# Attention inside a fused layer: a scaled projection moved to ScalarE and GpSimd, one more key block turned by VectorE, and the gather spread over all heads

## The chip, the cores and the metric

The kernel runs on one core of one Trainium2 chip. The metric is the time of one execution on the device, in microseconds (us). Besides that time there is one profiled execution, whose trace gives every instruction's start and duration on each engine: PE (TensorE; PEld is its weight load), DVE (VectorE), ACT (ScalarE), POOL (GpSimd) and SP (SyncE, which here only issues DMAs).

## What is computed

The reference takes x of 2 x 2048 tokens of width 256, normalises each token, and adds to x an attention (16 heads of width 64) and a mixture of experts (32 experts, 8 for each token, and a shared one):

```python
xn = _layernorm(x)
# attention
scores = jnp.einsum('bqhk,bshk->bhqs', Q, K) / jnp.sqrt(64)
attn   = jax.nn.softmax(scores, axis=-1)
out_h  = jnp.einsum('bhqs,bshk->bqhk', attn, V)
attn_out = jnp.einsum('bqhk,hdk->bqd', out_h, W_O) + b_O
# experts: the 8 best of 32 by sigmoid score, weights w normalised to 2.5
routed = sum over the 8 of w * down(silu(min(g, 7)) * clip(u, -7, 7))
shared = silu(xn @ shared_gate.T) * (xn @ shared_up.T) @ shared_down.T
return x + attn_out + routed + shared
```

All inputs are float32.

## The kernel before, in words

The program has three stages, each a block of five engine programs with a barrier at its end: `project_and_route` (Q, K and V, split into a high and a low part where scores need it, the routing, and a "base" of x, biases and shared expert, all written to device memory), `run_experts`, and `attend` (from L786), in which three quarters of the time goes.

`attend` walks over 2 batches x 16 heads x 16 query tiles of 128 queries, 512 slots in all. `slots` (L852) says what each slot does, `over_heads` (L874) unrolls head 0 and head 15 of each batch and runs heads 1 to 14 in a loop of one head a trip. Four tiles make a group (`GT`). The engines work on different tiles at one time. In a slot s:

- PE: `transpose` (L1033) turns the last 4 key blocks (`TURNED`) of the probabilities of tile s-2 into PSUM bank 7 (`TURN_BANK`). `score` (L1013) makes the 128 x 2048 scores of tile s in two halves of 1024, with 8 matmuls. `project` (L1062) multiplies the output of a tile 13 slots back with W_O into the same bank 7. `times_v` (L1047) multiplies probabilities with V for a whole group of 512 queries: in each slot 4 of the 16 key blocks, in the order of quarters `PV_ORDER = (3, 0, 1, 2)`, so that the four slots of a group are its places 0 to 3. V is only 64 wide, so even key blocks use columns 0 to 63 of the array and odd ones 64 to 127 (`side = t % 2 * DH`, L1056).
- DVE: two maxima over 1024 scores (`maximum`, L1132), the negated maximum (L1141), then one `scalar_tensor_tensor` (L1178) that takes the projection out of bank 7, scales it by 1/sum and adds it to the accumulator `acc`, then `turn_blocks` (L1146), a 32x32 block transpose of the first 12 key blocks (`MOVED`). Once a group come the sum and its reciprocal (L1188, L1191).
- ACT: exp of the second half (`exponent`, L1099), the copy of the 4 turned blocks (`take`, L1092), exp of the first half, and once a group the copy of the finished output (L1124).
- SP: all loads of q, k, v and W_O, and `exchange` (L913): 16 DMAs a group that move DVE's 32x32 blocks between partitions. Keys are loaded twice a head, once for each half of the tiles (`next_k`, L895).
- POOL: a loop that gathers the 8 expert rows of each token tile from device memory (L959), scales and adds them (L980, L983). It runs by itself through batch 1's 16 tiles, which go into the accumulator of batch 1, and then batch 0's, which go by way of device memory; at the end of batch 0 POOL adds them and stores the output (L1003, L1005).

The order around the changed parts is set by waits. PE's `transpose` of a slot waits until the projection before it has been taken out of bank 7: `wait_pos(pe, added, ...)`. So it waits for DVE's L1178, which stands behind both maxima. ACT's second-half exp waits for the negated maximum; PE's second half of scores waits for that exp.

Of the kernel before, what the change touches and what calls it, by code (L numbers as in the profile page):

```python
# [13 lines left out]
P = 128  # L14
# [578 lines left out]
def run_experts(nc, io, scr, keep, ahead, start):  # L593
    with ExitStack() as stack:
# [27 lines left out]
        @block.sync  # L622
        def _(sp):
            def load(i):
                for q in range(2):
                    e = 2 * i + q
                    wait_apart(sp, turned, 2 * i + q - 1, sp_waits)
                    wait_apart(sp, gu_ready, 2 * i + q - 1, sp_waits)
                    wait_apart(sp, dn_kept, 2 * i + q - 1, sp_waits)
                    load_expert(sp, io, scr, ahead, e, q)  # L630


            load_k(sp, scr, start, 0, 0, 0)
            load_q(sp, scr, start, 0, 0, 0)
            with sp.Fori(1, E // 2) as i:
                load(i)
# [123 lines left out]
MOVED = 12  # L760
# [4 lines left out]
PV_ORDER = (3, 0, 1, 2)  # L765
# [14 lines left out]
def load_k(sp, scr, start, b, h, side):  # L780

    sp.dma_start(start["k_hl"][:, side, :].bitcast(F32), scr["k"][bass.ds(h * P, P), b * T:(b + 1) * T]
# [3 lines left out]
def attend(nc, io, scr, keep, ahead, start):  # L786
    with ExitStack() as stack:
# [9 lines left out]
        acc_last = ahead["xe"][:, 1, :, :]  # L797
# [4 lines left out]
        acc_first = m.sb("acc", [P, TILES - CAP // P, D])  # L802
        acc_second = m.sb("acc_second", [P, TILES, D])
# [8 lines left out]
        rows = ahead["gu"][:, :, :, :].rearrange("p q k o -> p (q k) o")  # L812
        rest = m.sb("rest", [P, D])
        rest_t = rows[:, 0:2, :]
# [18 lines left out]
        cleared = m.sem("cleared")  # L833
        added = m.sem("added")
        rest_loaded = m.sems("rest_loaded", 2)
        finished = m.sem("finished")
        stored = m.sem("stored")
        restarted = m.sem("restarted")
        out_stored = m.sem("out_stored")
        g_staged = m.sem("g_staged")  # L840
        g_base = m.sem("g_base")
        gathered = m.sem("gathered")
        g_step = m.sem("g_step")
        g_stored = m.sem("g_stored")
        sp_waits, pool_waits = m.sem("sp_waits"), m.sem("pool_waits")
        block = stack.enter_context(nc.Block())

        def acc(b, t):

            if b == 1:  # L850
                return acc_second[:, t, :]
            return acc_first[:, t, :] if t < TILES - CAP // P else acc_last[:, t - (TILES - CAP // P), :]  # L852

        def slots(b, h):


            head = b * H + h
            opens = b == 0 and isinstance(h, int) and h == 0
            for s in range(LAST if b == B - 1 and isinstance(h, int) and h == H - 1 else TILES):
# [6 lines left out]
                    s=s, head=head, tile=tile, scores=s < TILES,  # L866
# [22 lines left out]
        def _(sp):  # L889
# [5 lines left out]
            def next_k(b, h, side):  # L895
                head = b * H + h
                wait_apart(sp, late_scored, (head - 1) * TILES + (side + 1) * TILES // 2, sp_waits)
                load_k(sp, scr, start, b, h, side)

            def load_v(b, h, place):  # L900
                wait_apart(sp, pv_done, GT * ((b * H + h) * GROUPS - 1) + place + 1, sp_waits)
                quarter = PV_ORDER[place]
                tiles = slice(quarter * GT, (quarter + 1) * GT)
                sp.dma_start(v[:, tiles, :],
                             scr["v"][bass.ds(h, 1), :, b * NS + quarter * GT:b * NS + (quarter + 1) * GT, :]
                             .rearrange("a p t c -> p (a t) c")).then_inc(v_loaded[quarter], 16)

            def load_wo(b, h, side):
                wait_apart(sp, projected, (b * H + h) * TILES - TILES // 2 * (1 - side), sp_waits)
# [13 lines left out]
            def head_loads(b, h, before, following):  # L923

                next_q(b, h, 1)
                next_k(b, h, 1)
# [5 lines left out]
                load_wo(b, h, 0)  # L932
# [3 lines left out]
                if following is not None:  # L936
                    next_k(*following, 0)
                exchange(b, h, 1)
                if following is not None:
                    next_q(*following, 0)  # L940
                exchange(b, h, 2)
                load_wo(b, h, 1)

            for b in range(B):
                head_loads(b, 0, (b - 1, H - 1) if b else None, (b, 1))
                with sp.Fori(1, H - 1) as h:
                    head_loads(b, h, (b, h - 1), (b, h + 1))
                head_loads(b, H - 1, (b, H - 2), (b + 1, 0) if b + 1 < B else None)
            exchange(B - 1, H - 1, GROUPS - 1)
            for t in range(TILES):  # L950
                sp.wait_ge(added, (B * H - 1) * TILES + t + 1)
                sp.dma_start(io["out"][(NT - TILES + t) * P:(NT - TILES + t + 1) * P, :], acc(1, t)
                             ).then_inc(out_stored, 16)
# [3 lines left out]
        def _(pool):  # L957
            def gather(k):
                nc.gpsimd.indirect_dma_start(  # L959
                    out=rows[:, k % 4, :], out_offset=None, in_=scr["ye"][:, :],  # L960
                    in_offset=bass.IndirectOffsetOnAxis(ap=g_index[:, k:k + 1], axis=0),
                    bounds_check=SLOTS, oob_is_err=True).then_inc(gathered, 16)

            def routed(i, tile):

                nc.gpsimd.tensor_copy(g_index[:, :], keep["index"][:, bass.ds(tile, 1), :]
                                      .rearrange("p a k -> p (a k)"))
                nc.gpsimd.tensor_copy(g_gain[:, :], keep["gain"][:, bass.ds(tile, 1), :]
                                      .rearrange("p a k -> p (a k)")).then_inc(g_staged, 1)
                pool.dma_start(rest[:, :], scr["base"][:, bass.ds(tile, 1), :].rearrange("p a d -> p (a d)")  # L970
                               ).then_inc(g_base, 16)
                wait_apart(pool, g_staged, i + 1, pool_waits)
                for r in range(2):
                    for k in range(4 * r, 4 * r + 4):
                        gather(k)
                    if r == 0:
                        wait_apart(pool, g_base, i * 16 + 16, pool_waits)
                    wait_apart(pool, gathered, i * (K * 16) + (r + 1) * 64, pool_waits)
                    for k in range(4):
                        nc.gpsimd.tensor_scalar(rows[:, k, :], rows[:, k, :], g_gain[:, 4 * r + k:4 * r + k + 1],  # L980
                                                None, ALU.mult).then_inc(g_step, 1)
                        wait_apart(pool, g_step, i * (2 * K) + 8 * r + 2 * k + 1, pool_waits)
                        nc.gpsimd.tensor_tensor(rest[:, :], rest[:, :], rows[:, k, :], ALU.add).then_inc(g_step, 1)  # L983
                        wait_apart(pool, g_step, i * (2 * K) + 8 * r + 2 * k + 2, pool_waits)

            with pool.Fori(0, TILES) as n:
                routed(n, n + TILES)
                nc.gpsimd.tensor_copy(acc_second[:, bass.ds(n, 1), :].rearrange("p a d -> p (a d)"), rest[:, :]
                                      ).then_inc(restarted, 1)
                wait_apart(pool, restarted, n + 1, pool_waits)  # L990
            with pool.Fori(0, TILES) as n:
# [285 lines left out]
```

## Time and profile before

| | us |
|---|---|
| median of 3 runs (3310.57 to 3320.97) | 3310.79 |
| profiled execution, its own time | 3305.17 |
| profiled execution, span of the instructions | 3303.7 |
| PE busy | 3196.1 (97%) |
| DVE busy | 2766.0 (84%) |
| ACT busy | 1767.6 (54%) |
| POOL busy | 1120.0 (34%) |
| mean granted TensorE clock | 0.991 |

Busy time is the union of an engine's instructions. A matmul's end is modelled, so PE can look busy while it is held up for a few hundredths of a microsecond; the starts are measured, and the distance from one start to the next is what the reader can trust. An fp32 matmul leaves two records in the trace, an fp32r one a single record. "<-" names what ended an idle time.

### The profile page before, as it was taken

Reading aid. Unit: us, or ns where it says so; the run is one execution under the profiler, and the core shown is the slowest. Engines: PE = TensorE matmul, PEld = TensorE weight load, DVE = VectorE, ACT = ScalarE, POOL = GpSimd, SP = SyncE. Lnnn points to the kernel's source line nnn. Section 1 sums busy time; section 2 is a strip of 40 time slices with the busy share of each in tenths; the row PEclk is TensorE's granted clock in tenths of the full one; section 3 lists DMA queues with packets and bytes.
Section 4 is the critical chain, followed back from the end, with each engine's and each line's share of the span. In section 5 each row is a group of like instructions: output and inputs, shape, how many; then the busy total and the mean of one; then the engine's idle time right before and its main releaser. Section 6 shows DMA issues by size and latency. Waiting matters only on the chain.

```text
span 3303.7 us, 53774 instructions
## 1 busy us (share of the span) xinstructions
PE 3196.1 (97%) x14468; PEld 1707.0 (52%) x14468; DVE 2766.0 (84%) x3431; ACT 1767.6 (54%) x3013; POOL 1120.0 (34%) x1347
## 2 busy tenths in 40 slices
PE   7799999898899999999999999999999999999998
PEld 3355444555455555555555555555555555555554
DVE  7612444234999999999999999999999999999996
ACT  4312320344666666666666666666666666666663
POOL 4677770012554555555544444444000000000000
PEclk9899999998999999999999999999999999999999
DMA  8623886665999999999999999999999888889887
GB/s 300 265 70 117 310 268 153 223 228 169 250 257 251 265 250 258 247 258 254 257 257 255 253 256 255 255 252 274 253 228 229 221 229 228 233 228 229 226 224 184
DMA packets 348745, 777.70 MB, mean 235 GB/s; under 512 B 130541, under 2 KB 182520, under 8 KB 340112
## 3 DMA queue, kind: packets, MB, share of 16 engines
q1 hardware_dynamic: 315664, 708.30, 79.0%
q0 software_dynamic: 33024, 68.71, 7.8%
q8 instruction: 27, 0.44, 0.1%
q14 instruction: 30, 0.25, 0.0%
HBM read 238.22 MB, written 161.61 MB: 121 GB/s over the span
## 4 chain that ended last, share of the span: by engine, by line
DVE 38%; PE 28%; issue 6%; DMA 2%; SPq 2%; DVEq 1%; ACT 0%
DVE at_half_max L1136 21%; DVE at_blocks L1152 14%; PE at_ps L1028 11%; PE at_ps L1058 9%; PE at_ps L1041 4%; PE at_ps L1072 3%; DMA at_moved<-at_blocks 2%; SPq L919 2%; DVE at_acc_second L1178 1%; DVE at_acc L1178 1%; DVE at_neg_max L1141 1%; DVEq L34 1%; DVE at_total L1188 0%; DVE ahead_xe L1178 0%; DVE at_inv L1191 0%
## 5 line engine op out<-in xcount | busy, mean ns | idle before, releaser
L1108 ACT ACTIVATE at_prob<-at_ps,at_neg_max 128x1024 f32<-128x1024 f32 x1024 | 1145.0, 1118 | 903.1 <-DVE at_neg_max L1141 788.7
L1136 DVE TENSOR_REDUCE at_half_max<-at_ps 128x1 f32<-128x1024 f32 x1024 | 1205.9, 1219 | 10.2 <-PE at_ps L1028 7.3
L1152 DVE STREAM_TRANSPOSE at_blocks<-at_prob 128x1536 f32<-128x1536 f32 x512 | 905.5, 1769 | 0.3 <-DMA at_moved<-at_blocks 0.3
L1028 PE MATMUL at_ps<-ahead_k_hl,ahead_q_hh 128*128 128x512 f32 x2048 | 850.5, 415 | 17.2 <-ACT at_prob L1108 10.3
L1028 PE MATMUL at_ps<-ahead_k_hl,ahead_q_ll 128*128 128x512 f32 x2048 | 806.4, 394 | 0.0
L1058 PE MATMUL at_ps<-at_moved,at_v 128*64 128x512 f32 x3072 | 726.3, 593 | 8.3 <-DMA at_moved<-at_blocks 7.0
L1041 PEld LDWEIGHTS at_ps<-keep_ident,at_prob 128*128 128x128 f32 x2048 | 215.8, 141 | 436.6 <-DVE at_acc_second L1178 170.8
L1028 PEld LDWEIGHTS at_ps<-ahead_k_hl,ahead_q_hh 128*128 128x128 f32 x2048 | 387.3, 189 | 87.4 <-ACT at_prob L1108 15.1
L1028 PEld LDWEIGHTS at_ps<-ahead_k_hl,ahead_q_ll 128*128 128x128 f32 x2048 | 388.1, 190 | 67.4
L980 POOL TENSOR_SCALAR ahead_gu<-ahead_gu,at_g_gain 128x256 f32<-128x256 f32 x256 | 236.6, 924 | 453.1 <-DMA ahead_gu<-ye,at_g_index 413.5
L1058 PEld LDWEIGHTS at_ps<-at_moved,at_v 128*64 128x64 f32 x3072 | 220.4, 137 | 286.3 <-issue 220.4
L1041 PE MATMUL at_ps<-keep_ident,at_prob 128*128 128x128 f32 x2048 | 335.4, 286 | 15.8 <-DVE at_acc_second L1178 4.1
L1072 PE MATMUL at_ps<-ahead_dn,ahead_xe 128*64 128x256 f32 x2048 | 334.3, 405 | 4.0 <-DVE at_acc_second L1178 2.4
L1096 ACT COPY at_turned_sb<-at_ps 128x512 f32<-128x512 f32 x512 | 300.6, 587 | 38.1 <-PE at_ps L1041 26.9
L959 POOL DMA_INDIRECT ahead_gu<-ye,at_g_index x256 | 265.4, 1037 | 100.1 <-issue 70.9
L286 POOL DMA_INDIRECT xbuf<-pr_ebase,pr_stage_i x256 | 249.6, 975 | 100.3 <-issue 72.2
L1058 PE MATMUL at_ps<-at_turned_sb,at_v 128*64 128x512 f32 x1024 | 247.8, 602 | 2.6 <-issue 2.0
L983 POOL TENSOR_TENSOR at_rest<-at_rest,ahead_gu 128x256 f32<-128x256 f32 x256 | 187.7, 733 | 47.0 <-POOL ahead_gu L980 47.0
L1108 ACT ACTIVATION_READ_ACCUMULATOR at_prob<-at_ps,at_neg_max 128x1 f32 x1024 | 201.3, 197 | 0.0
L1072 PEld LDWEIGHTS at_ps<-ahead_dn,ahead_xe 128*64 128x64 f32 x2048 | 102.4, 135 | 190.3 <-issue 186.1
L1178 DVE SCALAR_TENSOR_TENSOR at_acc_second<-at_ps,at_inv,at_acc_second 128x256 f32<-128x256 f32 x256 | 123.8, 484 | 27.2 <-PE at_ps L1072 23.8
L1058 PEld LDWEIGHTS at_ps<-at_turned_sb,at_v 128*64 128x64 f32 x1024 | 68.7, 136 | 113.9 <-issue 105.8
(119 smaller groups left out, 2287.4 us busy)
## 6 DMA issues: line engine op xcount, KB each, us to landing
at_moved<-at_blocks SPq DMA_DIRECT2D x2048, 192.0 KB
ahead_k_hl<-k_parts SPq DMA_DIRECT2D x64, 1024.0 KB, 8.2
ahead_q_hh<-q_parts SPq DMA_DIRECT2D x128, 256.0 KB
ahead_q_ll<-q_parts SPq DMA_DIRECT2D x128, 256.0 KB
xbuf<-pr_zeros SPq DMA_DIRECT2D x32, 512.0 KB, 5.1
q_parts<-pr_part_hi SPq DMA_DIRECT2D x64, 256.0 KB
q_parts<-pr_part_lo SPq DMA_DIRECT2D x64, 256.0 KB
k_parts<-pr_part_hi SPq DMA_DIRECT2D x64, 256.0 KB, 2.2
```

Source lines behind the costliest of these rows:

```text
L286: nc.gpsimd.indirect_dma_start(out=scr["xbuf"][:, :], out_offset=bass.IndirectOffsetOnAxis(ap=stage_i[:, q, k:k + 1], axis=0), in_=stage_x ...
L959: nc.gpsimd.indirect_dma_start(out=rows[:, k % 4, :], out_offset=None, in_=scr["ye"][:, :], in_offset=bass.IndirectOffsetOnAxis(ap=g_index ...
L980: nc.gpsimd.tensor_scalar(rows[:, k, :], rows[:, k, :], g_gain[:, 4 * r + k:4 * r + k + 1], None, ALU.mult).then_inc(g_step, 1)
L1028: last = nc.tensor.matmul(ps[:, bank, :], q[:, g % 2, j * P:(j + 1) * P], k_hl[:, side, c * CH:(c + 1) * CH], start=first, stop=not first)
L1041: last = nc.tensor.transpose(ps[:, TURN_BANK, j * P:(j + 1) * P], prob[:, s["s"] % 2, t * P:(t + 1) * P], keep["ident"][:, :])
L1058: last = nc.tensor.matmul(ps[side:side + DH, PV_BANK, :], v[:, t, :], p_T, start=(place == 0 and j < 2), stop=(place == GT - 1 and j >= GT ...
L1072: last = nc.tensor.matmul(ps[side:side + DH, TURN_BANK, 0:D], oT[:, g % 2, j * P + side:j * P + side + DH], wo[:, g // 2, :], start=True, ...
L1096: nc.scalar.copy(turned_sb[:, parity, :, :, j, :], ps[:, TURN_BANK, :].rearrange("p (t r c) -> p t r c", r=QD, c=32)).then_inc(copied, 1)
L1108: nc.scalar.activation(prob[:, i % 2, half * 1024:(half + 1) * 1024], ps[:, banks[0]:banks[1], :].rearrange("p b c -> p (b c)"), ACT.Exp, ...
L1136: nc.vector.tensor_reduce(half_max[:, i % 2, half:half + 1], ps[:, banks[0]:banks[1], :], AX.XY, ALU.max).then_inc(max_step, 1)
L1152: nc.vector.transpose(blocks[:, parity, :, j, :, :].rearrange("p c t k -> p t c k"), prob[:, (s["s"] - 1) % 2, 0:MOVED * P].rearrange("p ( ...
L1178: nc.vector.scalar_tensor_tensor(out=acc(of, t), in0=ps[:, TURN_BANK, 0:D], scalar=inv[:, t:t + 1], in1=acc(of, t), op0=ALU.mult, op1=ALU. ...
```

## The change

- `project` is unchanged, but its result is taken out of bank 7 by ACT (`scale_out`: scaled by 1/sum into `scaled_sb`, 128x256), as the first thing ACT does in a slot, and added to `acc` by POOL. PE's `transpose` now waits for `scaled`, ACT's step. DVE's `scalar_tensor_tensor` is gone, and so are its two memsets at the start.
- `MOVED` goes from 12 to 13: DVE turns 13 key blocks, PE 3; ACT's copy has 384 columns instead of 512; each exchange DMA carries 13/12 of the bytes. The four places of `times_v` take key blocks 13-15, 0-4, 5-8 and 9-12.
- The keys of a head are loaded once, in two DMAs of half the keys; buffers alternate between heads. W_O is loaded once a head too.
- POOL's gather is tied to the slots: one of the token tiles of the batch in each head; gathers in slots 0 to 7, scaling and adding straight into `acc` in slots 8 to 15. The base is loaded into `acc` ahead. One accumulator serves both batches; batch 0's tiles are stored and its buffers loaded again around the end of batch 0.
- `over_heads` runs 7 trips of two heads instead of 14 of one; POOL now uses it too.

```diff
-MOVED = 12
+MOVED = 13
-PV_ORDER = (3, 0, 1, 2)
+PV_PLACES = ((13, 16), (0, 5), (5, 9), (9, 13))
...
-                with eng.Fori(1, H - 1) as h:
-                    for s in slots(b, h):
-                        body(b, h, s)
+                with eng.Fori(0, H // 2 - 1) as i:
+                    for u in (1, 2):
+                        for s in slots(b, (i, u)):
+                            body(b, (i, u), s)
...
     def transpose(s):
...
-                    wait_pos(pe, added, s["out"][0] * GT + s["out"][2])
+                    wait_pos(pe, scaled, s["out"][0] * GT + s["out"][2])
...
     def times_v(s):
-                for j in range(GT):
-                    t = quarter * GT + j
+                for t in tiles:
                     side = t % 2 * DH
...
     def project(s):
-                wait_pos(pe, added, n)
+                wait_pos(pe, scaled, n)
...
+            def scale_out(s):                       # ScalarE, first in its slot
+                act.wait_ge(projected, n + 1)
+                if j == 0:
+                    act.wait_ge(inv_done, group + 1)
+                wait_pos(act, added, n - 1)
+                nc.scalar.activation(scaled_sb[:, t % 2, :], ps[:, TURN_BANK, 0:D], ACT.Identity,
+                                     scale=inv[:, t:t + 1]).then_inc(scaled, 1)
...
-                    nc.vector.scalar_tensor_tensor(out=acc(of, t), in0=ps[:, TURN_BANK, 0:D], scalar=inv[:, t:t + 1],
-                                                   in1=acc(of, t), op0=ALU.mult, op1=ALU.add
-                                                   ).then_inc(added, 1)
...
     # GpSimd, in each slot with an output
+                    wait_apart(pool, scaled, n + 1, pool_waits)
+                    nc.gpsimd.tensor_tensor(acc[:, t, :], acc[:, t, :], scaled_sb[:, t % 2, :], ALU.add
+                                            ).then_inc(added, 1)
...
     # GpSimd, routed(b, s): the gather of head h's token tile
+                if s["s"] < K:
+                    nc.gpsimd.indirect_dma_start(out=row(k), ...).then_inc(gathered[part], 16)
+                    return
+                if k % (K // 2) == 0:
+                    wait_apart(pool, gathered[part], n * 64 + 64, pool_waits)
+                nc.gpsimd.tensor_scalar(row(k), row(k), g_gain[:, k:k + 1], None, ALU.mult).then_inc(g_scaled, 1)
+                nc.gpsimd.tensor_tensor(into, into, row(k), ALU.add).then_inc(g_added, 1)
```

## Rows read from the trace of the kernel before

**Rows 1.** Stretches: us, busy PE, PEld, DVE, ACT, POOL; clock, DMA share, GB/s.
```profile
1000.00:1500.00 500.00, 495.27 (x2485) 266.15 (x2485) 491.73 (x568) 309.34 (x543) 263.76 (x324) 1.00 1.01 255
2500.00:3000.00 500.00, 496.76 (x2495) 267.57 (x2494) 493.08 (x572) 310.99 (x546) 0.00 (x0) 1.00 0.89 228
```
**Rows 2.** The page's chain that ended last, and line 1141's instances (ns, first and last).
```profile
DVE 38%; PE 28%; issue 6%; DMA 2%; SPq 2%; DVEq 1%; ACT 0%
...
L1141 DVE TENSOR_SCALAR at_neg_max<-at_half_max x512: 212/215/216, 807.3 to 3266.9; 128x1 f32<-128x1 f32 x171
```
**Rows 3.** Waits from 2500 to 3000 us: who for whom, us, times, longest.
```profile
ACT at_prob L1108 <- DVE at_neg_max L1141: 182.5, 104, 2.0
PEld at_ps L1041 <- DVE at_acc_second L1178: 80.1, 92, 1.1
PEld at_ps L1058 <- ACT ahead_xe L1124: 2.0, 7, 0.3
```
**Rows 4.** Timeline of one slot, 2416 to 2422 us: start, us, engine, line.
```profile
2416.56 0.66 PE L1041 MATMUL at_ps<-keep_ident,at_prob 128*128 128x128 f32 x4
2416.97 0.47 PE L1028 MATMUL at_ps<-ahead_k_hl,ahead_q_hh 128*128 128x512 f32 x1
2418.99 0.65 PE L1072 MATMUL at_ps<-ahead_dn,ahead_xe 128*64 128x256 f32 x4
2419.48 1.89 PE L1058 MATMUL at_ps<-at_moved,at_v 128*64 128x512 f32 x8
2420.74 0.49 DVE L1178 SCALAR_TENSOR_TENSOR at_acc_second<-at_ps,at_inv,at_acc_second 128x256 f32<-128x256 f32 x1
2421.14 1.77 DVE L1152 STREAM_TRANSPOSE at_blocks<-at_prob 128x1536 f32<-128x1536 f32 x1
2421.29 0.66 PE L1041 MATMUL at_ps<-keep_ident,at_prob 128*128 128x128 f32 x4
```
**Rows 5.** PE's timeline in the opening, before DVE has any projection to take.
```profile
851.48 0.66 PE L1041 MATMUL at_ps<-keep_ident,at_prob 128*128 128x128 f32 x4
...
853.91 1.94 PE L1058 MATMUL at_ps<-at_moved,at_v 128*64 128x512 f32 x8
855.77 0.44 PE L1041 MATMUL at_ps<-keep_ident,at_prob 128*128 128x128 f32 x2
```
**Rows 6.** PE's timeline from 2405.05 to 2405.09 us: what starts within 0.04 us.
```profile
2405.07 0.65 PE L1058 MATMUL at_ps<-at_turned_sb,at_v 128*64 128x512 f32 x2
```
**Rows 7.** PE's timeline in the experts' stage: full-width fp32 matmuls, one at a time.
```profile
703.16 3.69 PE L726 MATMUL ex_ps<-ex_xeT,ahead_gu 128*128 128x512 f32 x8
706.70 1.04 PE L716 MATMUL ex_ps<-keep_ident,ahead_xe 128*128 128x128 f32 x8
```
**Rows 8.** The page's costliest groups: shape xcount, busy us, mean ns, idle before.
```profile
L983 POOL TENSOR_TENSOR at_rest<-at_rest,ahead_gu 128x256 f32<-128x256 f32 x256 | 187.7, 733 | 47.0 <-POOL ahead_gu L980 47.0
```
**Rows 9.** DMA waits of the whole run, and issues (KB each, us to landing).
```profile
PEld at_ps L1058 <- DMA at_moved<-at_blocks: 12.7, 11, 4.4
...
ahead_k_hl<-k_parts SPq DMA_DIRECT2D x64, 1024.0 KB, 8.2
```
**Rows 10.** Timeline of attend's first microseconds, and of its fourth slot.
```profile
800.84 0.77 PE L1028 MATMUL at_ps<-ahead_k_hl,ahead_q_hh 128*128 128x512 f32 x1 [6.83 <-PEq L594]
801.36 2.62 DVE L1160 MEMSET at_acc<- 128x3072 f32 x1 [9.85 <-PEq L594]
804.97 2.29 DVE L1136 TENSOR_REDUCE at_half_max<-at_ps 128x1 f32<-128x1024 f32 x2
...
820.34 0.21 DVE L1141 TENSOR_SCALAR at_neg_max<-at_half_max 128x1 f32<-128x1 f32 x1
824.52 0.21 DVE L1141 TENSOR_SCALAR at_neg_max<-at_half_max 128x1 f32<-128x1 f32 x1
```
**Rows 11.** The end of the run.
```profile
3301.06 0.48 DVE L1178 SCALAR_TENSOR_TENSOR at_acc_second<-at_ps,at_inv,at_acc_second 128x256 f32<-128x256 f32 x1 [0.76 <-PE at_ps L1072]
```
**Rows 12.** The instruction queue of the page.
```profile
q8 instruction: 27, 0.44, 0.1%
```

More of the change, by code:

```diff
@@ L630, in load @@
                     load_expert(sp, io, scr, ahead, e, q)
-            load_k(sp, scr, start, 0, 0, 0)
+            for part in range(2):
+                load_k(sp, scr, start, 0, 0, 0, part)
             load_q(sp, scr, start, 0, 0, 0)
@@ L865, in slots @@
                 yield dict(
-                    s=s, head=head, tile=tile, scores=s < TILES,
+                    s=s, h=h, head=head, tile=tile, scores=s < TILES, side=side, pair=pair,
+                    out_side=1 - side if s < OUT_LAG else side, out_pair=pair - 1 if s < OUT_LAG and not side else pair,
                     turn=(head * GROUPS + back[0], back[0] % 2, (s - 1) % GT) if turn and s <= TILES else None,
@@ L893, in next_q, with next_k @@
                 load_q(sp, scr, start, b, h, g)
[L895 to L898, printed above, removed]
+            def next_k(b, h, side, part):
+                wait_apart(sp, late_scored, (b * H + h - 1) * TILES, sp_waits)
+                load_k(sp, scr, start, b, h, side, part)
             def load_v(b, h, place):
                 wait_apart(sp, pv_done, GT * ((b * H + h) * GROUPS - 1) + place + 1, sp_waits)
[L902 to L906, printed above, removed]
+                first, end = PV_PLACES[place]
+                sp.dma_start(v[:, first:end, :],
+                             scr["v"][bass.ds(h, 1), :, b * NS + first:b * NS + end, :]
+                             .rearrange("a p t c -> p (a t) c")).then_inc(v_loaded[place], 16)
             def load_wo(b, h, side):
-                wait_apart(sp, projected, (b * H + h) * TILES - TILES // 2 * (1 - side), sp_waits)
+                wait_apart(sp, projected, (b * H + h - 1) * TILES + 1, sp_waits)
                 sp.dma_start(wo[:, side, :], io["wo"][bass.ds(h, 1), :, :].rearrange("a p d -> p (a d)")
@@ L921, in exchange, with store_out, head_loads @@
                                      ).then_inc(exchanged[g % 2], 16)
-            def head_loads(b, h, before, following):
+            def store_out(b):
+                for t in range(TILES):
+                    sp.wait_ge(added, ((b + 1) * H - 1) * TILES + t + 1)
+                    sp.dma_start(io["out"][(b * TILES + t) * P:(b * TILES + t + 1) * P, :], acc[:, t, :]
+                                 ).then_inc(out_stored, 16)
+            def head_loads(b, h, side, before, following):
                 next_q(b, h, 1)
-                next_k(b, h, 1)
                 if before is not None:
@@ L940, in head_loads @@
                     next_q(*following, 0)
+                    next_k(*following, 1 - side, 1)
                 exchange(b, h, 2)
-                load_wo(b, h, 1)
             for b in range(B):
[L945 to L948, printed above, removed]
+                head_loads(b, 0, 0, (b - 1, H - 1) if b else None, (b, 1))
+                with sp.Fori(0, H // 2 - 1) as i:
+                    for u in (1, 2):
+                        head_loads(b, 2 * i + u, u % 2, (b, 2 * i + u - 1), (b, 2 * i + u + 1))
+                head_loads(b, H - 1, 1, (b, H - 2), (b + 1, 0) if b + 1 < B else None)
             exchange(B - 1, H - 1, GROUPS - 1)
[L950 to L953, printed above, removed]
+            store_out(B - 1)
             sp.wait_ge(out_stored, TILES * 16)
@@ L957, in _ @@
         def _(pool):
[L958 to L984, printed above, removed]
@@ L1017, in score @@
                         pe.wait_ge(q_loaded[g % 2], 32 * (head * 2 + g // 2) + 32)
[L1018 to L1019 removed]
+                    if i == 0:
+                        pe.wait_ge(k_loaded[side], 32 * s["pair"] + 32)
                     wait_pos(pe, early_exp, tile - 1)
@@ L1046, in times_v @@
                 group, g, place = s["pv"]
-                quarter, parity = PV_ORDER[place], g % 2
+                parity = g % 2
+                tiles = range(*PV_PLACES[place])
                 if place == 0:
```

151 lines of the change are left out of this document (81 added, 70 removed).

## The prediction

> **What bounds the kernel now.** I read the stages first. The attention runs at full clock and, over 500 us, PE is busy 496.76 and DVE 493.08 us with 104 slots' work in it [rows 1, 3]: both are full, ACT and POOL are not. Then the pace: the negated maximum comes 512 times between 807.3 and 3266.9 us [rows 2], so a slot takes 2459.6 / 511 = 4.81 us. The chain of waits gives DVE 38% and PE 28% [rows 2]: it passes to and fro. The waits say where they meet: PE's transpose stands behind DVE's projection step (92 of 104 slots) and ACT behind the negated maximum [rows 3].
>
> The timeline gives what each would need alone. PE, start to start: transposes 2416.56, scores 2416.97, projection 2418.99, V 2419.48, next transposes 2421.29 [rows 4], so 0.41 + 2.02 + 0.49 + 1.81 = 4.73 us. Is the 1.81 held up by DVE, whose step ends at 2421.23? The opening answers: without any such step V takes 853.91 to 855.77, 1.86 us [rows 5], no less. So 4.73 is PE's own time, and DVE costs 4.81 - 4.73 = 0.08 us a slot. DVE's own is 493.08 / 104 = 4.74 [rows 1, 3]. Two engines with the same period; taking work off one alone can give no more than 0.08 x 512 = 41 us.
>
> **The change, part by part.**
>
> *DVE.* The projection step goes: start to start it holds DVE 0.40 us (2420.74 to 2421.14) [rows 4]. The 13th block adds 1.77 / 12 = 0.15 us [rows 4]. New: 4.74 - 0.40 + 0.15 = 4.49 us a slot. DVE is no longer a bound; it then costs nothing as long as PE needs over 4.49.
>
> *PE, the wait.* Transposes now wait for ACT's scaling. The projection ends 0.49 us after 2418.99, and ACT has next to do the exp that waits for the maximum 1.75 us a slot (182.5 / 104) [rows 3]. A scaling of 256 columns takes at most the 0.59 us between two PE stages of that order; I have no row of that shape, its neighbour in work is DVE's 0.49 [rows 4]. It starts about 1.8 us before the transposes, so it is hidden unless it exceeds that. The 0.08 us goes: between 0 and -0.32 us a group of four slots, taken at -0.32.
>
> *PE, transposes.* Three instead of four. Two take 0.44, four 0.66 [rows 5]: 0.11 each, -0.44 us a group.
>
> *PE, times V.* This is the step that decides. A block's fp32 matmul is two records; the eight records of four blocks start two at a time [rows 6], an even and an odd block side by side in the two halves of the array. So four blocks are two rounds. A record's step is (1.89 - 0.65) / 3 = 0.41 us within V [rows 4, 6], and (706.70 - 703.16) / 8 = 0.44 us for full-width matmuls with nothing beside them [rows 7]. I take 0.43, so a round is 0.86 us whether one block is in it or two. The new places hold 3, 5, 4 and 4 blocks. Three (13, 14, 15) are an odd-even pair and an odd one alone: two rounds, as long as four blocks were. Five (0 to 4) are three rounds. After the lone block stands no even or odd partner but the next slot's transposes, which use the full width. A group needs 9 rounds instead of 8: +0.86 us. The bounds: 0, if a lone block takes half a round or overlaps what follows, and 0.88 (two records at 0.44).
>
> *The Trainium skill* ("TensorEngine Tiling (Array Packing)", Theoretical Speedup) gives a factor of up to 2 where the stationary side is at most 64 wide. Counted for each block, 16 blocks cost the same however they are grouped, the +0.86 would be nothing, and the result would be the first rival's. Counted as the trace shows it, a lone block gets no factor.
>
> *Sum for the slots.* Per group -0.32 - 0.44 + 0.86 = +0.10 us; 128 groups: +13 us. PE's four slots: 3 of 4.62 and one of 5.48. DVE, 4.49 on the average with the sums of a group in it, fits.
>
> *ACT* gets about 0.5 us a slot and loses a quarter of its copy. It is busy 310.99 us of 500 [rows 1], 3.0 of 4.81 us a slot: cover is there. Where it is near: V's place 0 waits for the copied output of the group before; PE already waits 2.0 us in 500 there [rows 3]. Between 0 and 0.3 us a group (the longest such wait), so 0 to 38 us. Since exp can come up to 4.81 - 4.49 = 0.3 us earlier against PE once DVE is ahead, I take 1 us in all.
>
> *POOL* adds 0.73 us a slot [rows 8] and keeps its gather, now over all 32 heads. At 263.76 us of 500 with the gather dense [rows 1], the new load is below 4.8 us a slot. A gather has four slots, 19 us, before it is used. ACT waits for an addition two slots back. Cost 0; if a gather came later than 19 us, ACT would stand and with it PE. The final additions for batch 0 and its stores fall away.
>
> *DMA and SP.* Keys: 64 transfers of 1 MB, 8.2 us each [rows 9], become the half. The exchanges grow by 1/12. Both are some 33 MB, so the load stays at a share of 0.89 to 1.01 [rows 1]. SP passes the second half of the keys just ahead of a group's exchange, a whole group before they are used, in place of the second load of the same head. All DMA waits of V are 12.7 us, 11 times [rows 9]. An exchange has about four slots, 19 us, from its blocks to the first use; if it fills them, a twelfth more is 1.6 us. I take +3 us in all (a few of the 128 waiting), bounds -5, as half the keys' traffic frees its queue, and +40.
>
> *Start.* DVE's memsets hold its first maximum to 804.97, though PE began at 800.84 [rows 10]: between 0 and -2.1 us, taken -1.5. The first eight slots are DVE's (824.52 - 820.34 = 4.18 us each [rows 10]): +0.15 x 8 = +1.2.
>
> *End.* The last step is DVE's at 3301.06 [rows 11]; now ACT's and POOL's 0.73 [rows 8] follow one another: +1. Behind the last scores there are two more groups' third rounds: +1.7.
>
> Total: 13 + 1 + 3 - 1.5 + 1.2 + 2.7 = +19 us. On the profiled execution's 3305.2 this is 3324; the median of the runs is 5.6 us above it, so 3330 us.
>
> **The rivals.**
>
> *The lone block is free.* Then a group gives -0.76 us, 128 of them -97, and the other terms leave 3310.8 - 97 + 6 = 3220 us, faster. For it: half the array is idle then, and a block alone moves half the work. Against: full-width matmuls alone step at 0.44 too [rows 7]; nothing in the step shrinks when the partner is missing. If only one of two lone blocks hid, nothing would change, since the three-block place costs no more than now.
>
> *ACT becomes the late one (slower still).* Scaling and output copy stand in one queue; V's place 0, 0.11 us earlier in its slot than now, waits each time. At 0.3 us a group +38: 3368 us. It decides as soon as exp starts no earlier against PE than now.
>
> *The loops fetch instructions anew.* A trip is now two heads long. The page shows 27 fetch packets, 0.44 MB, for the whole run [rows 12], so the loop of one head is kept. If two heads aren't, each of 14 trips pays between 0 and the 6.83 us that PE stood at the stage's start [rows 10]; at half of that +48: 3378 us. *The Trainium skill* ("Runtime: NRT & Kernel Launch", Instruction fetch mechanics) says that a taken branch to outside the held window of two 16 KiB pages stalls until the page is fetched, with 128 KiB for PE. PE's 384 matmul records a head and as many weight loads are over 48 KiB; by two pages the kernel before would refetch in each trip, and the 27 packets speak against that; by 128 KiB two heads just fit.
>
> **How the numbers follow.** Forecast 0.64, for which the own range is 3312 to 3352. Lone block free 0.13; ACT late 0.09; fetches 0.06; the remaining 0.08 a sum near zero, with V's third round partly hidden or the rest smaller than taken. About 0.3% (10 us) is what a measurement can tell from no change: faster is below 3301, slower above 3321. Faster 0.13 + 0.02 = 0.15. Same: 0.06 of the remainder and 0.13 of the forecast's low end, 0.19. Slower 0.66. The range 3300 to 3370 leaves out the first rival, half of the fetch case and the tails.
>
> **What would show it.** In the changed profile: V's place with five blocks takes 2.67 us to the next transposes and the one with three 1.8; transposes take 0.30; PE's transposes no longer wait for an engine; the slots pace 4.62, 5.48, 4.62, 4.62; DVE's busy share falls to 93% and it idles for PE's scores; ACT idles less. It is wrong if the five-block place takes under 2.4 us, if the group's period differs from 19.35 by over 0.2 us, or if a wait for ACT, POOL or a DMA stands before PE in each group.

## The result and the profile after

The changed kernel takes 3386.9 us (median of 4 runs, 3383.09 to 3398.47) against 3310.68 before: 1.0235 times, 95% interval 1.0216 to 1.0255, 76 us slower. The forecast was 3330. The sign was right and the size a quarter of what came; the time lies 17 us above the range. The profiled execution has a span of 3396.9 us against 3303.7, +93.2.

Where it lies: the negated maxima of the changed kernel run from 802.9 to 3356.4 us, 2553.5 us instead of 2459.6 [rows 2]. So +93.9 lie in the attention's slots, -4.4 ahead of them and +3.7 behind. The 512 starts of that line can be taken by head (16 slots). Before, most of the 30 heads behind the first take 77.0 to 77.5 us. Now an undisturbed head takes 77.4, and the heads in the loops take, in batch 0,

```
79.2 82.7 | 77.8 84.8 | 79.1 85.2 | 79.0 87.1 | 78.8 77.5 | 81.6 84.9 | 77.8 77.4     (heads 1 to 14)
```

What these 14 have above 77.4 is 49 us, and the 14 of batch 1 have 29 us. A loss once a trip of two heads, then, beside slots that are as forecast. One head outside the loops is long too: the first of batch 1 takes 84.2 us (76.6 before), 6.5 of them in a single slot.

First the slots, in the chain of waits, in order of time (start, us, what):

```profile
2568.61 0.48 PE at_ps L1056 x3
2569.09 1.83 PE at_ps L1043 x8
2570.92 0.58 PE at_ps L1088 x4
2571.50 2.57 PE at_ps L1073 x10
2574.07 0.48 PE at_ps L1056 x3
2574.55 1.85 PE at_ps L1043 x8
2576.40 0.58 PE at_ps L1088 x4
2576.99 1.72 PE at_ps L1073 x8
2578.70 0.48 PE at_ps L1056 x3
```

The chain is PE alone (L1056 transposes, L1043 scores, L1088 projection, L1073 V). The slot with five blocks takes 2574.07 - 2568.61 = 5.46 us, the next one 4.63. Five blocks take 0.85 more than four (2.57, 1.72): a lone block costs a whole round. The page's chain and stretch, and two groups:

```profile
PE 65%; DMA 3%; issue 3%; SPq 2%; DVE 2%; ACT 1%; ACTq 0%; POOL 0%; DVEq 0%; POOLq 0%
...
L1003 POOL TENSOR_TENSOR at_acc<-at_acc,at_scaled 128x256 f32<-128x256 f32 x512 | 370.7, 724 | 1153.6 <-ACT at_scaled L1136 1153.6
L1136 ACT ACTIVATE at_scaled<-at_ps,at_inv 128x256 f32<-128x256 f32 x512 | 242.9, 474 | 416.2 <-PE at_ps L1088 384.8
...
q8 instruction: 78, 1.28, 0.2%
q14 instruction: 102, 0.83, 0.1%
```

```profile
2500.00:3000.00 500.00, 490.13 (x2314) 256.49 (x2311) 446.14 (x454) 332.85 (x629) 209.53 (x262) 0.99 0.96 231
```

DVE went from 38% of the chain to 2% and from 493 to 446 us busy in 500 [rows 1, 2]; ScalarE's step is 0.474 us and waits for PE, in the chain shown above never PE for it. New are the last two lines: q8 moved 78 packets of instructions, where there were 27 [rows 12], and q14 102, where there were 30. q8 is taken for PE's and q14 for the other engines': with PE alone written out (e4) q8 moves 106 and q14 stays at 101, and with ScalarE written out as well (e10) q14 falls to 69.

Now a jump back, in the timeline of batch 0 (PE and ACT; in brackets the idle time ahead and what ended it):

```profile
1515.06 1.89 PE L1073 MATMUL at_ps<-at_moved,at_v 128*64 128x512 f32 x8
1524.18 0.90 PE L1056 MATMUL at_ps<-keep_ident,at_prob 128*128 128x128 f32 x3 [7.23 <-issue]
1525.12 0.48 ACT L1112 COPY at_turned_sb<-at_ps 128x384 f32<-128x384 f32 x1 [7.50 <-PE at_ps L1056]
```

PE stands 7.23 us and nothing but its own issue ends it. In batch 1 it looks different:

```profile
2644.24 1.89 PE L1073 MATMUL at_ps<-at_turned_sb,at_v 128*64 128x512 f32 x6
2649.53 0.47 ACT L1136 ACTIVATE at_scaled<-at_ps,at_inv 128x256 f32<-128x256 f32 x1 [5.40 <-issue]
2650.05 0.90 PE L1056 MATMUL at_ps<-keep_ident,at_prob 128*128 128x128 f32 x3 [3.93 <-ACT at_scaled L1136]
```

Here ScalarE stands at its own issue, at the first instruction of a trip, and PE waits for it. Both kinds can be followed by a lower granted clock (all six jumps of batch 0 are, and four of the six of batch 1), the third column from the end of these stretches (the columns are span, then busy time and count of PE, PEld, DVE, ACT and POOL, granted clock, and what DMA did):

```profile
2640.00:2650.00 10.00, 6.13 (x29) 2.68 (x25) 7.33 (x9) 3.94 (x9) 2.39 (x3) 0.99 0.88 202
2650.00:2654.00 4.00, 3.95 (x13) 3.06 (x15) 1.30 (x2) 2.67 (x5) 2.14 (x4) 0.60 1.00 255
2654.00:2664.00 10.00, 10.00 (x50) 5.14 (x50) 8.49 (x8) 6.42 (x12) 3.48 (x4) 1.00 1.03 238
```

There are 12 such gaps of PE, at the 6 jumps back of each batch. From the last record of V to the first transpose, start to start, they are 3.0 to 7.8 us in batch 0 and 2.5 to 4.6 in batch 1, 56 us together, 50 without the 0.52 that this pair of instructions always has. The slot behind a gap, start to start of PE's transposes, is longer by 1.3 to 2.8 us at the ten jumps with the lower clock and by 0.01 us at the two without it (2491 and 2808 us): 18 us more.

### The profile page after: what moved, and what is told of

It is laid out like the page before. It is cut to its first block, busy times and chain, and to the rows that moved or that the text cites. A ratio compares the mean times of both kernels' runs of the same rounds, so it can differ in the third digit from the quotient of the medians.

```text
span 3396.9 us, 53673 instructions
## 1 busy us (share of the span) xinstructions
PE 3250.8 (96%) x13955; PEld 1692.5 (50%) x13956; DVE 2606.3 (77%) x2917; ACT 1930.4 (57%) x3525; POOL 1454.0 (43%) x1795
## 4 chain that ended last, share of the span: by engine, by line
PE 65%; DMA 3%; issue 3%; SPq 2%; DVE 2%; ACT 1%; ACTq 0%; POOL 0%; DVEq 0%; POOLq 0%
PE at_ps L1073 26%; PE at_ps L1043 25%; PE at_ps L1088 8%; PE at_ps L1056 7%; SPq L914 2%; DMA at_v<-v_rows 1%; DVE at_half_max L1164 1%; DMA at_moved<-at_blocks 1%; DVE at_blocks L1180 0%; ACT at_prob L1124 0%; ACT at_scaled L1136 0%; DVE at_neg_max L1169 0%; ACT ahead_xe L1152 0%; SPq L905 0%; ACTq L874 0%
## 5 line engine op out<-in xcount | busy, mean ns | idle before, releaser
L1180 DVE STREAM_TRANSPOSE at_blocks<-at_prob 128x1664 f32<-128x1664 f32 x512 | 974.1, 1902 | 2.5 <-DMA at_moved<-at_blocks 1.5
L1043 PE MATMUL at_ps<-ahead_k_hl,ahead_q_hh 128*128 128x512 f32 x2048 | 857.5, 419 | 18.2 <-ACT at_prob L1124 11.3
L1003 POOL TENSOR_TENSOR at_acc<-at_acc,at_scaled 128x256 f32<-128x256 f32 x512 | 370.7, 724 | 1153.6 <-ACT at_scaled L1136 1153.6
L1073 PE MATMUL at_ps<-at_moved,at_v 128*64 128x512 f32 x3328 | 840.9, 596 | 13.2 <-DMA at_moved<-at_blocks 7.0
L1043 PE MATMUL at_ps<-ahead_k_hl,ahead_q_ll 128*128 128x512 f32 x2048 | 813.7, 397 | 0.0
L1136 ACT ACTIVATE at_scaled<-at_ps,at_inv 128x256 f32<-128x256 f32 x512 | 242.9, 474 | 416.2 <-PE at_ps L1088 384.8
L1073 PEld LDWEIGHTS at_ps<-at_moved,at_v 128*64 128x64 f32 x3328 | 258.1, 138 | 369.4 <-issue 306.2
L1043 PEld LDWEIGHTS at_ps<-ahead_k_hl,ahead_q_hh 128*128 128x128 f32 x2048 | 391.4, 191 | 89.7 <-ACT at_prob L1124 16.9
L1043 PEld LDWEIGHTS at_ps<-ahead_k_hl,ahead_q_ll 128*128 128x128 f32 x2048 | 392.7, 192 | 69.0
L1056 PEld LDWEIGHTS at_ps<-keep_ident,at_prob 128*128 128x128 f32 x1536 | 161.3, 142 | 461.5 <-issue 425.2
L1088 PE MATMUL at_ps<-ahead_dn,ahead_xe 128*64 128x256 f32 x2048 | 340.9, 407 | 3.8 <-ACT at_scaled L1136 2.4
L1056 PE MATMUL at_ps<-keep_ident,at_prob 128*128 128x128 f32 x1536 | 283.1, 294 | 49.1 <-issue 28.0
L1112 ACT COPY at_turned_sb<-at_ps 128x384 f32<-128x384 f32 x512 | 242.7, 474 | 145.6 <-PE at_ps L1056 144.9
L1073 PE MATMUL at_ps<-at_turned_sb,at_v 128*64 128x512 f32 x768 | 243.4, 602 | 2.2 <-issue 2.0
L1088 PEld LDWEIGHTS at_ps<-ahead_dn,ahead_xe 128*64 128x64 f32 x2048 | 104.1, 135 | 190.0 <-issue 185.5
L979 POOL DMA_INDIRECT ahead_gu<-ye,at_g_index x128 | 133.8, 1045 | 115.0 <-POOL at_acc L1003 75.8
L979 POOL DMA_INDIRECT ahead_xe<-ye,at_g_index x128 | 131.6, 1028 | 108.7 <-POOL at_acc L1003 103.3
```

Source lines behind the costliest of these rows:

```text
L979: nc.gpsimd.indirect_dma_start(out=row(k), out_offset=None, in_=scr["ye"][:, :], in_offset=bass.IndirectOffsetOnAxis(ap=g_index[:, k:k + 1 ...
L1003: nc.gpsimd.tensor_tensor(acc[:, t, :], acc[:, t, :], scaled_sb[:, t % 2, :], ALU.add).then_inc(added, 1)
L1043: last = nc.tensor.matmul(ps[:, bank, :], q[:, g % 2, j * P:(j + 1) * P], k_hl[:, side, c * CH:(c + 1) * CH], start=first, stop=not first)
L1056: last = nc.tensor.transpose(ps[:, TURN_BANK, j * P:(j + 1) * P], prob[:, s["s"] % 2, t * P:(t + 1) * P], keep["ident"][:, :])
L1073: last = nc.tensor.matmul(ps[side:side + DH, PV_BANK, :], v[:, t, :], p_T, start=(place == 0 and t < tiles[0] + 2), stop=(place == GT - 1 ...
L1088: last = nc.tensor.matmul(ps[side:side + DH, TURN_BANK, 0:D], oT[:, g % 2, j * P + side:j * P + side + DH], wo[:, s["out_side"], :], start ...
```

## The experiments

Theory: a trip of two heads (some 1670 instructions of PE and 380 of ScalarE, by the records of the trace) is no longer held, and is fetched anew at each jump. Rivals: the new order of loads, ScalarE's new step, the gather's place. Each line compares with the kernel before on the same chip.

| | us | before | ratio, 95% interval |
|---|---|---|---|
| e1 all heads written out | 3523.70 | 3527.49 | 0.9991, 0.9972 to 1.0010 |
| e2 before, two heads a trip | 3609.76 | 3527.49 | 1.0225, 1.0201 to 1.0249 |
| e3 places of 2, 6, 4, 4 | 3499.17 | 3527.49 | 0.9901, 0.9877 to 0.9925 |
| e4 PE written out | 3568.08 | 3527.49 | 1.0098, 1.0074 to 1.0121 |
| e5 one head a trip | 3533.38 | 3536.34 | 0.9993, 0.9968 to 1.0018 |
| e6 e5 with 12 blocks | 3467.50 | 3536.34 | 0.9802, 0.9769 to 0.9834 |
| e7 e1 less one block | 3454.11 | 3536.34 | 0.9769, 0.9748 to 0.9791 |
| e8 before, written out | 3502.68 | 3536.34 | 0.9887, 0.9855 to 0.9920 |
| e9 the changed kernel | 3394.98 | 3307.10 | 1.0258, 1.0233 to 1.0283 |
| e10 PE and ACT written out | 3341.82 | 3307.10 | 1.0096, 1.0070 to 1.0121 |
| e11 e1 with 12 blocks | 3272.22 | 3307.10 | 0.9887, 0.9861 to 0.9913 |
| e13 as e1 | 3336.20 | 3314.94 | 1.0063, 1.0045 to 1.0081 |
| e14 as e5 | 3337.98 | 3314.94 | 1.0076, 1.0054 to 1.0099 |
| e15 as e6 | 3273.10 | 3314.94 | 0.9870, 0.9851 to 0.9889 |

e1 to e8 ran on chips on which all kernels were some 190 to 220 us slower: the first negated maximum comes at 987 to 1003 us there, not at 803 to 807, after a first stage in which ScalarE and VectorE wait for signals that come late; why is not known. Differences inside a chip count. But the kernel before loses some 25 us more on these chips than its variants do, so their ratios lie 0.7 to 0.8% lower than on the others (e1 and e13, e5 and e14, e6 and e15 are the same kernels).

**e1_flat and e13_flat_again**

```diff
-                with eng.Fori(0, H // 2 - 1) as i:
-                    for u in (1, 2):
-                        for s in slots(b, (i, u)): ...
+                for h in range(1, H - 1):
+                    for s in slots(b, h): ...
```

> The changed kernel with heads 1 to 14 of each batch written out one after the other on every engine instead of 7 trips of two heads; the same instructions and data. Fetch theory: the slots of an undisturbed head take 77.4 us (4.62, 5.48, 4.62, 4.62) and what the loop heads took above that, 49 us in batch 0 and 29 us in batch 1, is the refetch of the code at each jump back and the lower clock after it; it goes, and the time is 3387 - 70 = 3317 us, between 3308 and 3328. Rival (transfers): the stalls come from the exchanges, the values or the new order of loads and only happen to fall at head boundaries; the time stays above 3370.

> e1 again (the changed kernel, all heads written out), beside the kernel before with a profile. If the chip made the difference: on a chip where attend starts at 803 us 1.007 to 1.011 of before, as e10; on one where it starts at 989 us 0.999. If VectorE's, GpSimd's and SyncE's trips cost 1%: 0.999 on either.

The 12 gaps are gone and loop heads take 77.5 to 79.3 us, but for one of 81.8 in e13. Against before the loss falls from 76 us (the result above) and 88 (e9) to 21 (e13) or -4 (e1, on a chip of the other kind). The rival, above 3370, is out. e13 is 8 us above e1's band. What it has beyond the forecast's slots is seen in its waits (1000 to 3200 us):

```profile
PE at_ps L1071 <- DMA at_v<-v_rows: 14.7, 17, 3.5
PEld at_ps L1071 <- DMA at_moved<-at_blocks: 7.5, 10, 2.8
PE at_ps L1071 <- DMA at_moved<-at_blocks: 3.2, 3, 2.3
```

Most fall on the place of five blocks in the first group of a head (a mean of 6.03 us instead of 5.48 between negated maxima, one of 10.8 at the start of batch 1 included), whose values SP asks for behind an exchange's 16 DMAs. Not all 25 us are new: in three profiles of the kernel before PE waits 5.7, 16.6 and 18.2 us for exchanges in the same stretch.

**e2_before_two**

```diff
-                with eng.Fori(1, H - 1) as h:
+                with eng.Fori(0, H // 2 - 1) as i:
+                    for u in (1, 2):
+                        for s in slots(b, 2 * i + u): ...
```

> The kernel before with 7 trips of two heads instead of 14 of one, nothing else. Fetch theory: its trip is then as long as the changed kernel's (PE some 1730 instructions), so it stalls at each jump: 3311 + 50 to 80, about 3370 us, with several times the 27 packets of the instruction queue. Rival (the stalls belong to the new order of loads or to ScalarE's new step): 3311 us, 27 packets.

The old kernel, with nothing else changed (SP has the same trips), loses 82 us. Its loop heads in batch 0 take 79.7 to 87.1 us. The page's queue shows the refetch:

```profile
q8 instruction: 88, 1.44, 0.2%
```

This is the direct proof: the trips alone make the old kernel 2.25% slower, as much as the whole change did. But it is not the same engine that stands. Its waits (1000 to 3500 us):

```profile
PE at_ps L1043 <- issue: 25.1, 10, 4.8
DVE at_half_max L1138 <- issue: 23.1, 8, 3.6
```

In batch 0 PE stands at its own issue at the six jumps, as in the changed kernel. In batch 1 it is VectorE, 3.4 to 3.6 us at the first instruction of each later trip, and not ScalarE. By the records of the trace VectorE has 362 instructions in this trip and 258 in the changed kernel's, where it never stands so; ScalarE has 284 here and 381 there. The jumps are only part of this kernel's loss: its loop heads of batch 0 have some 78 us above 77.4, and the six slots with the jumps hold 34 of them. Where the rest comes from stays open.

**e4_flat_pe and e10_flat_pe_act**

```diff
-        def over_heads(eng, body):
+        def over_heads(eng, body, flat=False):   # flat: heads 1 to 14 written out
...
-            over_heads(pe, body)
+            over_heads(pe, body, flat=True)
```

e10 does the same for `act`.

> The changed kernel with only TensorE's program written out; ScalarE, VectorE, GpSimd and SyncE keep the trips of two heads. Fetch theory with two sources: batch 0's stalls (PE's own fetch, 4 to 8 us a trip) shrink to what ScalarE's fetch costs, 2.5 to 4.6 us a trip as in batch 1 now; 14 trips at about 3.5 = 49 us above e1: 3366 us if nothing of ScalarE's was hidden under PE's, between 3345 and 3370. Rival, all from PE's fetch: as e1. Rival, all from ScalarE's: as the changed kernel, 3387.

> e4 with ScalarE's program written out as well; VectorE, GpSimd and SyncE keep trips of two heads. Fetch theory with two sources: e4 had 1.0098 of before against e1's 0.9991, and the 38 us between them are ScalarE's code fetched at each jump; they go: 0.999 to 1.002 of before. Rival (VectorE's, GpSimd's or SyncE's trips stall too): stays at 1.005 or above.

> The changed kernel itself, beside the others on one chip: 1.0235 of before as measured, 1.020 to 1.026. All theories expect it; it is the measure for e4 and e10.

With PE written out 44 us above e1 are left (49 expected), and in e4's waits the stall is ScalarE's own and PE's behind it:

```profile
ACT at_scaled L1141 <- issue: 50.2, 13, 5.5
PE at_ps L1061 <- ACT at_scaled L1141: 32.9, 12, 4.1
```

With ScalarE written out too (e10), both lines are gone and the time is 53 us below the changed kernel on the same chip (e9). Its 1.0096 looked like the rival (other engines' trips), since e1 had 0.9991; e13 on a chip like e10's then had 1.0063. So most of that 1% was the chip's, not the trips'; up to 0.3% may be VectorE's, GpSimd's or SyncE's.

**e5_one_head and e14_one_head_again**

```diff
-                with eng.Fori(0, H // 2 - 1) as i: ...
+                with eng.Fori(1, H - 1) as h: ...
-                    next_k(*following, 1 - side, 0)
+                    next_k(*following, 0)        # and next_k(b, h, 1), load_wo(b, h, 1) as before
```

> The changed kernel with trips of one head again, which takes back with it the keys and W_O loaded once a head (a trip of one head cannot alternate buffers): keys and W_O twice a head as before. ScalarE's scaling, GpSimd's addition, 13 turned blocks in places of 3, 5, 4, 4 and the gather over all heads stay. Fetch theory: the trip fits again, no stalls at the jumps: as e1, 0.999 of before (0.996 to 1.004), some 27 packets in PE's instruction queue. Rival (the stalls came with GpSimd's and ScalarE's new steps or with the gather's place): 1.01 to 1.023 of before. Rival (the keys' doubled traffic is what costs): slower than e1 by over 10 us by waits for DMAs.

> e5 again (the changed kernel with one head a trip and keys and W_O twice a head). Forecast with the term of the trips taken out: a group of 19.35 us, 3330 less nothing: 1.004 to 1.008 of before on a chip with a start at 803 us. If keys once a head help, e13 is faster than this; if writing out costs by waits for DMAs, slower.

A trip of one head is held: 26 packets, no gap. e14's 3338.0 is within 2 us of e13 and 8 of the forecast. Keys once a head and writing out, the two differences between e13 and e14, together bring nothing that can be measured; what moves is what PE waits for (1000 to 3200 us): in e14 24.3 us for exchanges and 3.0 for values, in e13 10.7 and 14.7.

**e7_drop_block** (leaves key block 4 out of the product with V)

```diff
-                tiles = range(*PV_PLACES[place])
+                tiles = [t for t in range(*PV_PLACES[place]) if t != 4]
```

> e1 without the matmul of key block 4, the block that stands alone in the place of five; this part of the product with V is left out. Places of 3, 4, 4, 4: 8 rounds. Pair theory: a whole round of 0.86 us a group goes, 110 us, a little less if VectorE's 4.49 to 4.8 a slot shows: 0.968 to 0.973 of before. Rival (a lone block costs half a round and the rest of the long slot is a wait): -55 us, 0.983.

The long slot falls from a median of 5.48 us to 4.62, the whole round: the rival of a half round is out. The total fell by less than 110 us, by some 78 (0.9991 to 0.9769, outside the band): loop heads went from 78.2 us (e1) to 75.7 on average, not to 74. The rest turned into waits for values and exchanges. The slot of the values that come late goes from 5.9 us only to 5.6 on average, and the last long slot of a head from 5.4 to 4.8. The slots with DVE's sums take 4.67 to 4.82 in both.

**e3_even**

```diff
-PV_PLACES = ((13, 16), (0, 5), (5, 9), (9, 13))
+PV_PLACES = (((14, 16),), ((13, 14), (0, 5)), ((5, 9),), ((9, 13),))
```

> e1 with the four places holding 2, 6, 4 and 4 key blocks (14 and 15; 13 and 0 to 4; 5 to 8; 9 to 12), each an even number with both halves of the array, so that no block is alone. Pair theory: 8 rounds instead of 9 a group, -0.86 us x 128 = -110 us against e1: 3207 us, slots 3.76, 5.48, 4.62, 4.62. Rival (VectorE or the chain over ScalarE is just behind PE and takes over at 4.7 a slot): 3245 us or more. Rival (the third round is not the lone block's): as e1.

25 us better than e1, not 110: the first rival, and something more. Between negated maxima the short slot takes 4.57 us and the long one 5.18. But that is VectorE's clock. PE itself, from transposes to transposes, does the short slot in 3.84 us, nearly as forecast, and then takes 5.90 in the long one instead of 5.48. Once a group it stands there for banks that ScalarE's exp has to free, and the exp waits for the negated maximum (2500 to 3000 us):

```profile
PEld at_ps L1043 <- ACT at_prob L1124: 14.4, 25, 0.6
```

So the undisturbed slots give 51 us, and the slot of the late values, 7.1 us on average where e1 has 6.1, takes some 20 of them away again. What PE saves in a slot of 3.84 it waits for in the next, since each slot needs VectorE's two maxima.

**e6_one_head_12, e15_one_head_12_again and e11_flat_12**

```diff
-MOVED = 13
+MOVED = 12
-PV_PLACES = ((13, 16), (0, 5), (5, 9), (9, 13))
+PV_PLACES = ((12, 16), (0, 4), (4, 8), (8, 12))
```

> e5 with 12 key blocks turned by VectorE and 4 by PE, places of 4 as before: what is left of the change is the projection's way over ScalarE and GpSimd and the gather over all heads. Pair theory: a group takes 4 x 4.73 = 18.92 us instead of 19.35, so 55 us less than e5, and against before the 0.08 us of waiting a slot, 38 us, is gained: 0.986 of before (0.982 to 0.991). Rival (the wait for VectorE is replaced by one for ScalarE): as before, 1.00.

> e6 again (one head a trip, 12 turned blocks, places of 4): 4.76 us a slot, 55 to 66 us below e14. 0.980 on a chip with a start at 989 us, 0.988 to 0.990 on one with a start at 803 us, as e11 had.

> e1 with 12 turned blocks in four places of 4: all heads written out, keys and W_O once a head, ScalarE's and GpSimd's steps. Pair theory: 18.92 us a group instead of 19.35, -55 us against e1: 0.983 of before. If loading keys once is worth anything by itself, it is below e6's 0.980; if writing out costs (its code comes by DMA all the time), above.

With the 13th block taken back, 65 us go (e14 to e15), and the kernel is 1.3% faster than before: the best version, with e11. (e6's 0.9802 lies below its band, on a chip where the kernel before loses 25 us more.) Undisturbed heads fall from 77.5 to 76.2 us, some 40 us in all; the rest are waits for DMAs that a place of five blocks has and one of four has not. e15's stretch and chief waits:

```profile
2500.00:3000.00 500.00, 499.87 (x2520) 270.52 (x2519) 452.49 (x473) 364.32 (x657) 220.53 (x276) 1.00 0.97 244
```

```profile
PEld at_ps L1050 <- issue: 85.2, 105, 0.8
...
ACT at_prob L1118 <- DVE at_neg_max L1163: 65.7, 105, 0.7
```

PE's transposes (L1050) wait for no engine any more, where 92 of 104 did [rows 3]. PE now has no slack: 105 slots in 500 us, 4.76 each.

**e8_before_flat, e12_before_look and e16_before_look**

```diff
-                with eng.Fori(1, H - 1) as h:
+                for h in range(1, H - 1):
```

> The kernel before with all heads written out. Fetch theory: its one-head trip fitted, so nothing is gained: 0.998 to 1.002 of before. Rival (jumps cost in any loop, so that writing out flatters e1): 14 x 2 jumps at 1 us or more, 0.992 or less.

> The kernel before itself, for its profile on the chip of these runs: heads of 77.1 us as in the first trace plus what the later start and slower transfers of this chip add; no theory differs.

> The kernel before itself, for its heads on this chip. If the chip makes the difference, its heads on a chip with a start at 989 us take over 78 us on average in place of 77.1, by waits for DMAs.

By its time e8 goes to the rival, 34 us faster on its chip. By its trace it does not: the rival's microsecond at each jump is nowhere in the looped kernel, whose slot at the jump takes 4.82 us where e8's takes 4.73. Most of e8's heads in batch 1 take 76.1 us where the looped kernel's take 77.0 (e12 and e16), but those of batch 0 average 78.1 against 77.4 and 77.6. From the first to the last negated maximum e8 takes 2466.7 us, the looped kernel 2459.6 to 2469.0 in its three profiles, all on the other chips. So most of the 34 us may be what the looped kernel loses on chips like e8's. In batch 1 the slots with the sums take 4.83 us instead of 4.97, and PE's transposes no longer wait for VectorE (1000 to 3400 us):

```profile
PEld at_ps L1041 <- issue: 413.5, 486, 2.1
```

VectorE has 124 records a head written out and 182 looped; the difference is register arithmetic and waits. That this is what makes it quicker is likely and was not tried by itself. The other two profiles showed the first trace's heads again (3315.5 and 3309.0 us). Neither fell on a chip like e1's or e8's, so how the old kernel loses some 25 us more there than the others (212 and 221 against 188 to 195) stays open.

## Why the prediction was wrong

**What bounds the kernel: right.** PE's own slot was put at 4.73 us. Three of e15's four slots have a median of 4.73. With DVE relieved they do not get shorter. The fourth has 4.83, up to 4.96 in one group of a head; what holds it was not tried.

**The wait for VectorE: right, a little too dear.** Priced at 0.08 us a slot, up to 41 us. In e15, which has the old pairing, a slot takes 4.76 us instead of 4.81 to 4.83: the loop heads fall from 77.2 to 76.2 us, 31 us over all. That e15 is 42 us below before is closer to the 41 than the slots are.

**Transposes and lone block: right.** Slots of 4.62, 5.48, 4.62, 4.62 were forecast, and the medians are 4.62, 5.48, 4.62, 4.62. Taking the 13th block back gave 65 us, of which some 40 in undisturbed slots (55 by the sum). So this part of the change, meant for DVE, costs PE more than the transpose that it saves.

**ScalarE and GpSimd: right in the slots.** 0.474 us, between nothing and 0.59 (the 0.587 of ScalarE's copy of 512 columns in the page of before), and hidden. GpSimd's 0.72.

**DMA: mis-sized.** +3 us was taken, with a bound of 40. Between 1000 and 3200 us PE waits for exchanges and values 12 us in the changed kernel, 25 in e13 and 27 in e14, against 6 to 18 in three profiles of before. So with the gaps out of the way some 7 to 21 us come, within the bound. The place of five blocks needs more values at once, and they are asked for late.

**The passage between the batches: at nothing.** "The final additions for batch 0 and its stores fall away" was all that was said of it. In the changed kernel that place has one slot of 12.0 us, whose values come late (10.4 and 10.8 in e14 and e13, 6.2 in e15, 4.8 before): some 6 us. GpSimd stores batch 0's tiles and loads the base again just there; that this is the cause was not tried.

**Start and end: small, as forecast.** -1.5 + 1.2 + 2.7 was forecast. Measured -4.4 ahead of the first negated maximum, but three profiles of before differ by 3 us there; -1.9 in the first head, whose early slots take the 0.14 us more that was forecast; and +3.7 behind the last.

**The term that failed: the jumps.** The forecast's total has none for them. It stood among the rivals with a chance of 0.06 and a price of 48 us, as "The loops fetch instructions anew", and it is what happened: 53 us between the changed kernel and e10, 53 to 65 between its ratio and those of e13 and e14 (1.0235 and 1.0258 less 1.0063 to 1.0076, of 3310 us). The chance was wrong. The price was nearly right, in part by luck: it was 14 times half of a stand at the stage's start. There are 12 jumps, each costs PE 4.2 us on average, and the lower clock behind them, which the price did not have, 1.5 us more. Two readings misled. The 27 packets showed that one head is held, and I took that as evidence for two; it only excludes a window smaller than one head's trip. And I counted PE alone, at "over 48 KiB" a head for its matmuls and weight loads, and took twice that for still held. The trace shows PE refetching in batch 0 all the same and not in batch 1, with the same trip. ScalarE, which stalls in batch 1, I did not count at all: the change gives it 16 more steps and their waits a head, 191 records instead of 143, and twice the head. *The Trainium skill* ("Runtime: NRT & Kernel Launch", Instruction fetch mechanics) names 128 KiB for PE, 32 KiB for the other engines, and a stall at a jump out of the window. No run shows either size, but ScalarE's trip of some 380 records stalls here, and one of 190 does not, nor one of 284 in batch 1 of e2, where VectorE's of 362 does. With the measured 53 us in, the sum is 3330 + 53 = 3383 us, against 3386.9 measured: nothing else as large is missing.

Of the 78.5 us that the loop heads have above 77.4, 50 are PE's gaps and 18 the slots behind them, where the granted clock is at its lower level; some 10 are left for waits for values and exchanges. Gaps and clock make 68 us, and taking the jumps away gave 53 to 65. Some of it comes back as waits for DMAs, of which PE has 12 us in the changed kernel, 25 in e13 and 27 in e14.

## What to carry to other kernels

Before doubling a loop's body, count every engine's instructions in a trip, the ones that are not the bottleneck too, since an engine that PE waits for stalls PE as well. A page's count of instruction packets says what is held now, not how much more would be. And where a matmul uses half of the array's columns, work comes in pairs: count rounds in each stretch between full-width instructions, not blocks.

## What the runs showed that was not expected

- The same trip of two heads refetched PE's code in batch 0 and not in batch 1, where the loop stands elsewhere in the program: q8 has no packet between 2307 and 3285 us.
- Which engine stands at a jump follows its own count of instructions: in batch 1 ScalarE with 381 records a trip in the changed kernel, VectorE with 362 in e2.
- A stall can cost a second time: behind ten of the 12 gaps the granted clock is at its lower level (half) for some microseconds (2650 to 2654 us: 0.60 on average, matmuls of the scores at 0.63 us instead of 0.40), which makes the next slot 1.3 to 2.8 us longer.
- Writing heads out made the kernel before 1.1% faster on one chip (0.9887), though its loop was held; some 0.7% of that may be the chip's.
- An engine with 4.49 us of work a slot costs time where PE has a slot of 3.84, even when the next one is long: PE's two slots took 3.84 + 5.90 us against a forecast of 9.24.
